# Query and key length scaling moved to GpSimd per tile, with a padded stream and a new order of steps, in a fused adaLN, guidance and local attention block

## What is computed

```python
h = shift_token(x)                      # the upper 64 columns come from the row before
q, k, v = to_heads(h @ wqkv)            # 8 heads of 64
q = l2norm(q) * qs;  k = l2norm(k) * ksc
q, k = rotary_xpos(q, k)                # cos part + sin part of the half-turned vector
x = x + local_attention(8 * q, k, v) @ wo        # windows of 64, own window and the one before
h = shift_token(x)
h = (h - h.mean()) / sqrt(h.var() + 1e-5) * lg + lb
a, g = split(h @ w1 + b1)
x = x + (a * gelu(g)) @ w2 + b2
```

## Time and profile before

| | |
|---|---|
| median of 3 runs | 967.3 us (965.48 to 968.2) |
| the profiled execution's own time | 966.96 us |
| its span, first to last instruction | 965.0 us |
| mean granted clock of TensorE in it | 0.942 |
| instructions | 19306 |

### The profile page before, as it was taken

One profiled execution on the slowest core, in us unless ns is written; L12 is line 12 of the kernel. 1 busy time (PEld: TensorE's weight loads), 2 busy tenths in 40 slices (PEclk: granted clock), 3 DMA queues, 4 the chain that ended last, 5 costly groups with the idle time before them and its releaser, 6 DMA issues.

```text
span 965.0 us, 19306 instructions
## 1 busy us (share of the span) xinstructions
PE 786.4 (81%) x7151; PEld 556.3 (58%) x7151; DVE 668.0 (69%) x1588; ACT 659.3 (68%) x1545; POOL 539.6 (56%) x324
## 2 busy tenths in 40 slices
PE   4456788879889989888969979888888989888874
PEld 4334566656556666655657656656565666656543
DVE  4566876685687877586887967486787776676732
ACT  0234766867576985877786886877675887868672
POOL 2046853493956653394985643293966690576600
PEclk9668789999899999999999999999999999999997
DMA  6000000000000000000000000000000000000000
GB/s 206 0 12 1 12 2 1 1 1 2 1 2 1 23 2 22 2 1 1 1 1 2 23 1 23 1 2 1 1 1 2 12 2 13 2 1 2 1 1 22
DMA packets 12275, 9.85 MB, mean 10 GB/s; under 512 B 1040, under 2 KB 11288, under 8 KB 12184
## 3 DMA queue, kind: packets, MB, share of 16 engines
q1 hardware_dynamic: 12184, 8.64, 3.0%
HBM read 6.54 MB, written 2.10 MB: 9 GB/s over the span
## 4 chain that ended last, share of the span: by engine, by line
PE 40%; DVE 20%; ACT 19%; issue 11%; POOL 9%; DMA 0%; SPq 0%; POOLq 0%; ACTq 0%; DVEq 0%
ACT probs L964 7%; PE pair L696 6%; PE mixed L727 5%; POOL qk L1494 4%; PE dense L831 4%; PE pair L759 3%; DVE space L1393 3%; DVE q_norm L1398 3%; PE dense L795 3%; PE dense L796 2%; PE dense L797 2%; DVE qk L1195 2%; PE dense L908 2%; ACT squares L1083 2%; ACT probs_t L972 2%
## 5 line engine op out<-in xcount | busy, mean ns | idle before, releaser
L1494 POOL TENSOR_TENSOR qk<-space 128x512 f32<-128x512 f32 x128 | 186.4, 1463 | 58.0 <-DVE q_norm L1398 55.1
L1454 POOL TENSOR_TENSOR root<-power,minus_half 128x32 f32<-128x32 f32 x32 | 174.0, 5438 | 4.6 <-DVE power L1404 4.6
L964 ACT ACTIVATE probs<-pair,neg_max 128x128 f32<-128x128 f32 x512 | 138.3, 402 | 18.9 <-DVE neg_max L1215 18.5
L1393 DVE TENSOR_TENSOR space<-dense,tables 128x512 f32<-128x512 f32 x128 | 87.5, 684 | 36.9 <-ACT space L1087 35.2
L908 PE MATMUL dense<-wq_hi,h_hi 128*128 128x512 f32 x192 | 90.2, 470 | 26.6 <-DVE space L1393 10.9
L1491 POOL TENSOR_TENSOR space<-space,tables 128x512 f32<-128x512 f32 x64 | 82.7, 1293 | 50.7 <-ACT space L1087 50.7
L696 PE MATMUL pair<-eye_s,probs 128*128 128x128 f32 x512 | 80.9, 292 | 34.9 <-ACT probs L964 34.7
L1215 DVE TENSOR_REDUCE neg_max<-pair 128x4 f32<-128x512 f32 x128 | 82.0, 684 | 35.2 <-PE pair L759 35.1
L1083 ACT ACTIVATE squares<-dense 128x512 f32<-128x512 f32 x128 | 79.1, 618 | 39.5 <-PE dense L910 38.6
L696 PEld LDWEIGHTS pair<-eye_s,probs 128*128 128x128 f32 x512 | 59.1, 146 | 56.2 <-ACT probs L964 51.9
L1398 DVE TENSOR_REDUCE q_norm<-squares 128x8 f32<-128x512 f32 x128 | 86.4, 675 | 0.0
(11 more groups left out here) (166 smaller groups left out, 1809.2 us busy)
## 6 DMA issues: line engine op xcount, KB each, us to landing
x_in<-n_L_attn_embeddings_dram SPq DMA_DIRECT2D x8, 256.0 KB, 3.0
out_dram<-hn SPq DMA_DIRECT2D x8, 256.0 KB, 2.4
qk<-in_L_ffn_wqkv_dram SPq DMA_DIRECT2D x1, 1536.0 KB, 6.2
qk<-in_L_ffn_w_dram SPq DMA_DIRECT2D x1, 682.0 KB, 7.5
wo_s<-in_L_ffn_wo_dram SPq DMA_DIRECT2D x2, 256.0 KB
o_t<-in_L_wmod_dram SPq DMA_DIRECT2D x1, 384.0 KB, 3.3
probs<-const_rotary_dram SPq DMA_DIRECT2D x1, 256.0 KB, 3.6
band_s<-const_band_dram SPq DMA_DIRECT2D x1, 256.0 KB, 7.8
```

The lines of the kernel that those rows point to most:

```text
L964: last = act.activation(probs[:, ring, hh, :], banks[m][:, hh * P:(hh + 1) * P], ACT.Exp, bias=neg_max[:, ring, hh:hh + 1], scale=1.0)
L1393: dve.tensor_tensor(turned_s[:, t % 2, m, :].rearrange("p (h a b) -> p h a b", h=HEADS, a=2), halves[:, :, ::-1, :], rot(layer, t, 2 * m + 1),
L1454: return pool.tensor_tensor(to, of, minus_half[:, 0:of.shape[-1]], ALU.pow)
L1494: pool.tensor_tensor(qk[s][:, t, m * INNER:(m + 1) * INNER], turned_c[:, t % 2, m, :], turned_s[:, t % 2, m, :], ALU.add).then_inc(added, 1)
```

## The change

- `qk` is multiplied by the inverse lengths on POOL, one instruction per tile (128x1024), 64 in all; DVE's `unit_length` is gone.
- The inverse root of the 32 sums is no longer one power instruction: DVE makes half the sum and a first guess, POOL refines it in ten small instructions, each of which waits for the one before it.
- POOL's addition waits for the end of DVE's sine part and no longer for the sum of squares; the sum of squares is a step of its own (`norm`).
- The streams `y_new` and `y_t` have one zero column ahead, so the shifted stream is a view of them. `shifted` and ACT's `shift` are gone. DVE rounds in two casts; the rest is made by POOL for the lower and by DVE for the upper 64 partitions. In the feed forward PE takes eight float32 products of 64 columns in place of four transposes.
- The layer norm's weights are multiplied into `w1` and `b1` at the start. ACT then copies PE's second transpose rounded to `h_hi`, DVE subtracts for `h_lo`; one buffer pass, DVE's cast and POOL's part are gone.
- `v_cross` is filled by DMAs between buffers on SP's queue (two per pair of tiles, 64 in all), no longer by ACT; PE's `mix` of odd tiles waits for them.
- ACT rounds the projection weights in the set-up, which is made of steps of its own.
- Steps are finer (turn, flip, mix by half; up by bank) and stand in a new order.

```diff
 unit_root (POOL):
-inverse_root(root[:, :], power[:, :]).then_inc(qk_rooted, 1)
+pool.wait_ge(qk_seeded, pair_ + 1)
+count = NEWTON * pair_ + 1
+pool.tensor_tensor(root[:, 1, :], root[:, 0, :], half[:, :], ALU.mult).then_inc(qk_newton, 1)
+pool.wait_ge(qk_newton, count)
+for k in range(3):
+    pool.tensor_tensor(scratch[:, :], root[:, 0, :], root[:, 1, :], ALU.mult).then_inc(qk_newton, 1)
+    pool.wait_ge(qk_newton, count + 1)
+    pool.tensor_tensor(scratch[:, :], threes[:, :], scratch[:, :], ALU.subtract).then_inc(qk_newton, 1)
+    pool.wait_ge(qk_newton, count + 2)
+    if k < 2:
+        pool.tensor_tensor(root[:, :, :], root[:, :, :], scratch[:, :].rearrange("p (o h) -> p o h", o=1)
+                           .broadcast_to([P, 2, 32]), ALU.mult).then_inc(qk_newton, 1)
+        count = count + 3
+        pool.wait_ge(qk_newton, count)
+    else:
+        pool.tensor_tensor(root[:, 0, :], root[:, 0, :], scratch[:, :], ALU.mult).then_inc(qk_rooted, 1)
 unit (POOL, per tile):
+pool.wait_ge(added, 2 * tau + 2)
+pool.wait_ge(qk_rooted, 2 * before + t // 2 + 1)
+rows = qk[s][:, t, :].rearrange("p (h d) -> p h d", d=DH)
+pool.tensor_tensor(rows, rows, root[:, 0, 16 * (t % 2):16 * (t % 2) + 16].rearrange("p (h o) -> p h o", o=1)
+                   .broadcast_to([P, 2 * HEADS, DH]), ALU.mult).then_inc(qk_ready, 1)
 add (POOL):
-pool.wait_ge(summed, 2 * tau + m + 1)
+pool.wait_ge(*read_at(i, slot, (PROJ, "tile", t, m)))
 turn (PE):
-pe.wait_ge(qk_ready, 2 * before + t // 2 + 1)
+pe.wait_ge(qk_ready, tau + 1)
 feed forward stats (PE):
-done(turn_four(to, lambda k: flat(shifted)[:, k * P:(k + 1) * P]), i, slot, step)
+for k in range(TILES):
+    at = (k % 2) * P
+    for part in range(2):
+        last = pe.matmul(to[:, k * P + part * WIN:k * P + (part + 1) * WIN],
+                         y_t[stream(slot)][:, k // 2, at + 1 - part:at + 1 - part + P],
+                         eye_s[:, part * WIN:(part + 1) * WIN], start=True, stop=True)
 feed forward norm (ACT) and lo (DVE):
-act.activation(hn[:, :], src[:, :], ACT.Identity, scale=columns[...], bias=columns[...])
+act.activation(h_hi[:, :], bank(i, slot, step)[:, :], ACT.Copy).then_inc(ff_hi, 1)
+dve.tensor_tensor(h_lo[:, :], src[:, :], h_hi[:, :].bitcast(F32), ALU.subtract)
 projection hi (DVE):
-dve.tensor_copy(h_hi[:, :], flat(shifted)).then_inc(qkv_hi, 1)
+for rows, view in shifted_halves(proj_source(i, slot)):
+    last = dve.tensor_copy(by_seq(h_hi[rows, :]), view)
 values (ACT) and SP:
-act.activation(v_cross[s][half_rows, t // 2, :, 0:DH], heads[half_rows], ACT.Copy)
+sp.dma_start(v_cross[s][rows, p, :, :], v[s][rows, t, :, :]).then_inc(v_crossed[s][p], 16)
 the order on PE, slot 0 of a full turn:
-0:a.flip.2 0:proj.tile.0.0 0:proj.tile.0.1 0:proj.tile.0.2 0:a.mix.2 0:proj.tile.1.0
+0:ff.down 1:ff.stats 0:proj.tile.0.0 0:proj.tile.0.1 0:proj.tile.0.2 0:proj.tile.1.0
```

More of the change, by code:

```diff
@@ new lines @@
+        2:proj.norm.0.1 2:proj.tile.0.1 2:proj.tile.1.0 2:proj.norm.1.0 2:a.project 2:proj.tile.1.1
+        2:proj.norm.1.1 2:proj.root.0 2:proj.tile.2.1 2:proj.norm.2.0 2:proj.norm.2.1 2:proj.tile.2.0
+        2:proj.tile.3.0 2:proj.norm.3.0 2:proj.tile.3.1 2:proj.norm.3.1 2:proj.root.1 2:ff.lo 2:new.gate
+        2:new.again 2:ff.up.1 2:ff.up.0 3:a.score.0.0 3:a.score.0.1 3:a.score.1.0 3:a.score.1.1 2:ff.up.2
+        2:ff.down 2:new.stream 2:store.turn 2:proj.keep 3:a.mix.0.0 3:a.mix.0.1 3:proj.hi 3:proj.lo
@@ new lines @@
+        3:a.score.1.1 2:ff.up.2 2:ff.down 2:new.stream 2:store.turn 2:proj.keep 3:a.mix.0.0 3:a.mix.0.1
+        3:proj.hi 3:proj.lo 3:ff.stats 3:a.mix.1.0 3:a.mix.1.1 3:ff.norm 3:proj.tile.0.0 3:proj.norm.0.0
+        3:a.score.2.0 3:a.score.2.1 3:a.mix.2.0 3:proj.tile.0.1 3:a.mix.2.1 3:a.score.3.0 3:a.score.3.1
+        3:proj.norm.0.1 3:proj.norm.1.0 3:proj.tile.1.0 3:proj.tile.1.1 3:a.mix.3.0 3:a.mix.3.1
+        3:proj.norm.1.1 3:proj.root.0 3:proj.norm.2.0 3:proj.tile.2.1 3:proj.norm.2.1 3:proj.tile.2.0
```

1154 lines of the change are left out of this document (664 added, 490 removed).

## The result

| | before | changed |
|---|---|---|
| median of four runs each, us | 967.75 (965.48 to 968.42) | 1019.18 (1015.58 to 1023.72) |
| profiled execution, span, us | 966.96, 965.0 | 1023.72, 1021.9 |
| mean granted clock of PE | 0.942 | 0.931 |

The ratio is 1.0538, 95% interval 1.0491 to 1.0585: 51 us more, where 44 fewer were forecast and the range ended at 968. The profiled execution of the changed kernel was the longest of its four, 4.5 us above the median.

What follows compares the result with a forecast made beforehand. The kernel was taken to be bound by hand-over between engines, with PE as floor. From the 965 us span, -38 - 10 + 24 - 16 - 4 gave 921, or 923 with what lies around the span; range 882 to 968.

Steps and rivals of the forecast that it cites:

- The four gains: Feed forward and projection chains -38 us, lengths -10, ACT and DVE queues -16, start and end -4.
- Order, +24: Slot 0's twelve projection triples in one run: PE idles 5 us, then 3 for qk0, in each of four turns.
- the other slots: Slots that receive the work moved out of slot 0 gain from it, lowering the order's +32 us to +24.
- ACT "goes from 659 to about 578 us": ACT's busy time falls as the shifted and v_cross copies leave it and the h_hi copy gets lighter.
- Chains, -38: Feed forward and projection 3.2 us shorter per slot, 51 us over 16 slots, three quarters bare; bounds -15 and -51.
- Queues, -16: PE waits less for ACT (81 us lighter) and DVE (53 lighter) in the middle; bounds 0 and -35.
- Float32 products, +1.1 us each: In each feed forward, PE's eight float32 products take 1.8 us where four transposes took 0.67; bounds 0 and +2.9.
- Lengths, -10: Inverse root and multiply per tile on POOL, additions not waiting for the sum of squares: -0.6 us per slot.
- The signs: What the new profile would show if right: ACT near 580 us, DVE near 615, POOL 580 to 620, twelve slots some 600.
- Rival (b): POOL becomes the bound through root and multiplies ahead of a.turn; 987 us at 4 us bare per slot; chance 0.12.
- Rival (c): Path not shortened: freed ACT and DVE time is slack, the run costs the feed forward's gain; 967 us, chance 0.06.

Runs made afterwards that it cites:

- e1: The changed kernel's instructions put in the order of the kernel before: 968.5 us, ratio 1.0011 to the kernel before.
- e13: e1 with statistics by eight half transposes (957.3 us), plus slots 2 and 3's norm copied into hn by ACT and split later by DVE: 955.8 us.
- e15: e1 with statistics by eight half transposes (957.3 us), plus both halves of the projection's h_lo on DVE, none on POOL: 955.4 us.
- e2: e1 with slot 0's twelve projection triples in one run behind the output projection, slot 1's statistics ahead of them: 1017.0 us, ratio 1.0532.

## Why the prediction was wrong, step by step

The forecast of 923 us missed the 1019.2 by 96: some 69 of these are gains that didn't come, 27 are the order. The gains decide. Had they come as priced, the order's 50.7 us would still have left some 950, inside the range.

- **The four gains, -38 - 10 - 16 - 4 = -68: measured +1.4** (e1 against the kernel before beside it). This is the step that failed first. I took time off ACT's, DVE's and POOL's work and counted a fixed share of it as bare, three quarters for the chains. In e1, ACT has 73.8 us less work and PE stands still only 16.7 us less, while PE's own work, which is the floor, grew by 15.0. v_cross -9.8, products +11.2 and lengths about +3 leave some -3 for the removed shifts and the folded norm weights, where some 40 us of ACT left. Why this gave so little stays open; e13 and e15 exclude two places, and e1's translated table, which nobody tuned for shorter steps, is a third that no run tested.
- **Order, +24 (bounds 0 and +48): 50.7 us.** This is the other step that failed; one edit, the run, makes 48.4 in the old order. The price of the waits, 8 us in each of four turns, came out right in sum, e2 has 8.0 more, and partly by luck: in slot 1's gaps banks of the run make 2.5 of them, the wait for `hn` ahead of it, which I had not seen, 2.7, and `qk0` behind it 1.8, where I had 5 and 3. Two things around it were wrong. I subtracted 8 us for "the other slots", which were to gain from the work moved to them; none did (slot 0 of e2 has 1.8 us more waiting in sum, slots 2 and 3 have 3 us more time). And I put it at nothing that PE itself works more slowly in such an order, 3.8 us per turn. In the changed kernel's run of turn 2, 15.6 us stand against 8.4 + 5.
- **ACT "goes from 659 to about 578 us": 623.5.** The new instructions do bring it to 585.5 (e1). I read the new order for PE and DVE but never followed which table ACT needs from step to step. 25 loads more, 32 us of ACT, are visible in the listing alone: `ff.up` stands between two `a.score`. Taking 30 loads out gives 13.4 us.
- **Chains, -38, with three quarters bare.** Added work costs a third by way of the chain (6.7 of 20 us) and 13.9 us by way of ACT's queue; removed work gave next to nothing.
- **Queues, -16, for 81 us off ACT and 53 off DVE.** The `v_cross` copies alone are worth 9.8 us. DVE lost only 19.0 us in e1 and 2.8 in the changed kernel: half and seed of the root took 31.4 and 56.9 us, where the sum had 6 more than 10.6.
- **Float32 products, +1.1 us each.** Measured +20.0 us of PE's time in the changed kernel, 1.25 each; 11.2 us of the time in the old order, none that could be told in the new.
- **Lengths, -10.** Single costs were right or cautious (258 ns against 0.24 to 0.31 us, multiply 1.90 against 2.4). The gain isn't there, since PE hardly waited for either version: 2.2 us in all before, 1.0 after. If anything the sign is the other one.
- **The signs.** ACT near 580, DVE near 615 and POOL at 580 to 620 us came out as 623.5, 665.2 and 527.8. Twelve slots, which were to take 600 us, take 695.3 from addition to addition, 638.9 in the kernel before and 642.8 in e1.
- **Rival (b)** (slower, 0.12) has the sign, and is right that DVE's small instructions would pay (330 ns became 807 and 972), but e1, with 525 and 455, is no slower than before, and POOL did not become the bound. The loss came from no rival of mine. **Rival (c)** is right for e1 in one half, that the freed time of ACT and DVE is slack; its other half, that the run costs only what the feed forward gains, is wrong.

## What to carry to other kernels

An order that puts a long piece of one kind in one run can have waits at three places: ahead of it, for a bank that an earlier step still holds; in it, for the engines that empty its banks; and behind it, for what is made from it. Price each, and expect PE's own busy time to grow (28.3 us for the same instructions here, about half of it by the clock); subtract nothing for the place that the piece left, unless a wait there is seen to end. Time taken off an engine that isn't the floor is no gain until a run shows it. When an order is changed, follow each engine's hidden state as well as its queue; on ACT, write the table behind every step and count the changes. And test "is it bare" with the same added work before and behind the consumer, because the added work alone answers for the queue too.
